# A fused attention and expert step: q and k turned by four transposes, and the score operands laid out by DMAs

## The reference

```python
x = x + 0.5 * ffn(layernorm(x))          # shared expert (2048 wide) and 8 routed experts, top 2
x = x + attn(layernorm(x))
x = x + 0.5 * ffn(layernorm(x))
# attn: groups of 64 tokens, 16 heads of 16 features
q, k, v = split(x @ w_qkv)
q, k = rmsnorm(q) * ln_w, rmsnorm(k) * ln_w
att = softmax(where(causal, q @ k.T / 4, -max))   # per group and head, 64 x 64
y = (att @ v) @ w_proj
```

## Time and profile before

| | before |
|---|---|
| median of three runs | 2153.27 us |
| span of the profiled execution | 2152.2 us |
| PE matmul busy | 2122.4 us |
| PE weight loads busy | 1945.3 us |
| DVE busy | 1428.8 us |
| ACT busy | 1031.8 us |
| POOL busy | 461.3 us |
| DMA moved | 168.41 MB, mean 78 GB/s |

### The profile page before, as it was taken

The page is one execution under the profiler, slowest core; times in us unless marked ns, Lnnn a source line. Parts: engine busy times, 40 slices in busy tenths (PEclk is TensorE's granted clock), DMA queues, the critical chain, the costliest instruction groups (busy, mean ns, idle before and its releaser), DMA issues.

```text
span 2152.2 us, 38420 instructions
## 1 busy us (share of the span) xinstructions
PE 2122.4 (99%) x14228; PEld 1945.3 (90%) x14228; DVE 1428.8 (66%) x3140; ACT 1031.8 (48%) x2006; POOL 461.3 (21%) x440
## 2 busy tenths in 40 slices
PE   9999999999999999999999999999999999999999
PEld 7888899999998888888888888888999999988888
DVE  7666656666665788888888987666466666633333
ACT  4233335555553666666666663333355555532222
POOL 2423211212122222222224322332112121200000
PEclk9999999999999999999999999999999999999999
DMA  9231225564445000000101102221244444441010
GB/s 271 103 110 64 68 74 135 131 148 104 101 112 150 21 2 20 21 20 1 36 1 57 38 11 88 91 83 57 70 104 105 109 104 104 111 135 60 30 59 20
DMA packets 194602, 168.41 MB, mean 78 GB/s; under 512 B 17017, under 2 KB 175149, under 8 KB 194416
## 3 DMA queue, kind: packets, MB, share of 16 engines
q1 hardware_dynamic: 176752, 144.57, 22.5%
q0 software_dynamic: 17664, 21.38, 5.7%
HBM read 104.32 MB, written 68.07 MB: 80 GB/s over the span
## 4 chain that ended last, share of the span: by engine, by line
PE 85%; DVE 9%; issue 3%; ACT 1%; SPq 1%; POOL 0%; DMA 0%; another core or an unknown queue 0%; DVEq 0%; ACTq 0%
PE gate_up_p L339 28%; PE quad L339 24%; PE out_p L377 21%; PE misc L377 4%; PE misc L512 2%; PE quad L529 1%; DVE p_s L1178 1%; PE misc L403 1%; DVE smax L1174 1%; PE quad L543 1%; DVE h_s L1042 1%; PE misc L395 1%; DVE y_s L1187 1%; PE misc L414 1%; PE misc L412 1%
## 5 line engine op out<-in xcount | busy, mean ns | idle before, releaser
L339 PE MATMUL gate_up_p<-zh,w 128*128 128x512 f32 (+2 forms) x2368 | 703.4, 360 | 0.6 <-DVE zl L1346 0.5
L713 ACT CAST hh<-h_s 128x512 fp32r<-128x512 f32 (+2 forms) x511 | 276.3, 541 | 700.4 <-DVE h_s L1042 631.9
L339 PE MATMUL quad<-zh,w 128*128 128x512 f32 (+2 forms) x1728 | 481.8, 346 | 0.0
L339 PEld LDWEIGHTS gate_up_p<-zh,w 128*128 128x128 f32 x2368 | 428.3, 188 | 48.7 <-DVE zl L1346 0.9
L377 PE MATMUL out_p<-w,hh 128*128 128x256 f32 x2808 | 455.5, 281 | 3.3 <-DVE hl L1058 1.9
L377 PEld LDWEIGHTS out_p<-w,hh 128*128 128x128 f32 x2808 | 400.8, 188 | 23.5 <-DVE hl L1058 4.4
L339 PE MATMUL gate_up_p<-zl,w 128*128 128x512 f32 (+2 forms) x1184 | 420.3, 355 | 0.0
L1058 DVE TENSOR_TENSOR hl<-h_s,hh 128x512 fp32r<-128x512 f32 (+2 forms) x431 | 247.2, 574 | 136.4 <-ACT hh L713 118.9
L1042 DVE TENSOR_TENSOR h_s<-gate_up_p,sg_s 128x512 f32<-128x512 f32 (+2 forms) x296 | 178.4, 603 | 236.5 <-PE gate_up_p L339 217.4
L339 PEld LDWEIGHTS quad<-zh,w 128*128 128x128 f32 x1728 | 308.5, 188 | 24.6
L339 PE MATMUL quad<-zl,w 128*128 128x512 f32 (+2 forms) x864 | 295.3, 342 | 0.0
(11 more groups left out here) (201 smaller groups left out, 2747.6 us busy)
## 6 DMA issues: line engine op xcount, KB each, us to landing
stage<-in_L_ffn_rg SPq DMA_DIRECT2D x128, 128.0 KB
stage<-in_L_ffn_ru SPq DMA_DIRECT2D x128, 128.0 KB
stage<-in_L_ffn_rd SPq DMA_DIRECT2D x128, 128.0 KB
slots_d<-empty SPq DMA_DIRECT2D x16, 662.5 KB, 7.5
zh_d<-zh SPq DMA_DIRECT2D x16, 512.0 KB
zl_d<-zl SPq DMA_DIRECT2D x16, 512.0 KB
y_d<-x SPq DMA_DIRECT2D x16, 512.0 KB
zh<-zh_d SPq DMA_DIRECT2D x16, 512.0 KB, 4.1
```

Source lines behind the costliest of these rows:

```text
L339: last = pe.matmul(dst, a, b, start=(k == 0), stop=(k == 3 * n - 1))
L713: nc.scalar.copy(hh[:, n % 2, 0:ncol], h_s[:, n % 2, 0:ncol]).then_inc(sm["hh_done"], 1)
```

## The change

q and k are turned as plain 128 x 128 blocks: four transposes (`head_transposes`) straight from `qk` into `quad` bank 0, after `up` of the same step in which `qk_normal` ran. ACT rounds the bank into `qkh` (`heads_high`, after the cast of the turned probabilities), DVE subtracts for `qkl` (`heads_low`, before `pl`). SP writes both to a scratch in DRAM, eight DMAs per tile, each part where the layout of the score operands has it (q as high, low, high, low and k as high, high, low, low, 16 rows each per head), and loads `k_t` and `q_t` from there by four DMAs once the scores of the tile before are done. The score products keep their number. `qcat`, `kcat`, `twin`, `queries`, both `k_t` copies and POOL's two subtractions go. The scores stand after the second `gate` in every step and wait for the loads and for `heads_low` of the tile that is in stage z, since both use `quad` bank 0. `qk_normal` stands before `values_low` in every step. SP's waits and DMAs of the fused stretch are written out by steps (`fused`), with the saves and loads of heads at the end of each.

```diff
+        heads_d = dram("heads_d", [2, 2, HALF_HEADS, PARTS, HD, C], F32)
...
-        q_t = sb("q_t", [P, NH // 2, 2, P], F32R, att)
-        qcat = sb("qcat", [P, NH, 64], F32, att)
-        kcat = sb("kcat", [P, NH, 64], F32, att)
+        q_t = sb("q_t", [P, NH // 2, 3, GROUP], F32R, att)
+        qkh = sb("qkh", [P, 2, C], F32R, att)
+        qkl = sb("qkl", [P, 2, C], F32R, att)
...
-            def pair_transposes(src, rows, done):
+            def head_transposes(t):
+                pe.wait_ge(sm["a_qn"], t + 1)
+                for j in range(2):
+                    for k in range(KC):
+                        o = j * C + k * P
+                        last = pe.transpose(quad[:, 0, o:o + P], qk[:, j, k * P:(k + 1) * P], ident[:, :])
+                last.then_inc(sm["a_qkt"], 1)
+
+            def prob_transposes(t):
+                pe.wait_ge(sm["a_exp"], t + 1)
+                wait(pe, sm["a_pl"], t)
                 for j in range(NH // 2):
-                    last = pe.transpose(misc[0:rows, j // 4, (j % 4) * P:(j % 4 + 1) * P],
-                                        src[:, 2 * j:2 * j + 2, :].rearrange("p h d -> p (h d)")[:, 0:rows], ident[:, :])
-                last.then_inc(sm[done], 1)
+                    last = pe.transpose(misc[:, j // 4, (j % 4) * P:(j % 4 + 1) * P],
+                                        p_s[:, 2 * j:2 * j + 2, :].rearrange("p h d -> p (h d)"), ident[:, :])
+                last.then_inc(sm["a_pt"], 1)
 
             def scores(t, z, out):
-                pe.wait_ge(sm["a_qe"], t + 1)
-                pe.wait_ge(sm["a_ke0"], t + 1)
-                pe.wait_ge(sm["a_ke1"], t + 1)
+                pe.wait_ge(q_in[t % 2], 32 * (t // 2 + 1))
+                pe.wait_ge(k_in[t % 2], 32 * (t // 2 + 1))
                 if z is not None:
-                    pe.wait_ge(sm["a_qn"], z + 1)
+                    pe.wait_ge(sm["a_qkl"], z + 1)
                     pe.wait_ge(sm["a_vl"], z + 1)
                 if out is not None:
                     pe.wait_ge(sm["a_o"], out + 1)
@@ -526,7 +541,8 @@
                     o = (j % 4) * P
                     for g, rows in ((1, P), (0, GROUP + 2)):
                         own = slice(GROUP * g, GROUP * g + GROUP)
-                        last = pe.matmul(quad[0:rows, j // 4, o:o + P].rearrange("p (r c) -> p r c", r=2), q_t[:, j, g, 0:rows],
+                        last = pe.matmul(quad[0:rows, j // 4, o:o + P].rearrange("p (r c) -> p r c", r=2),
+                                         q_t[:, j, g:g + 2, :].rearrange("p a c -> p (a c)")[:, 0:rows],
                                          k_t[:, j, :, own], start=(g == 1), stop=True, skip_group_check=(g == 0))
                 last.then_inc(sm["a_s"], 1)
 
@@ -552,15 +568,9 @@
...
-                if uses:
-                    pe.wait_ge(sm["misc_free"], max(uses) + 1)
...
-                if keys is not None:
-                    pe.wait_ge(sm["a_qlo"], keys + 1)
-                    wait(pe, sm["a_pl"], keys - 1)
-                    pair_transposes(qcat, QKROWS, "a_qt")
...
-                if keys is not None:
-                    pe.wait_ge(sm["a_qe"], keys + 1)
-                    pair_transposes(kcat, QKROWS, "a_kt")
                 if z is not None:
                     qkv(z, out)
...
                 if probs is not None:
-                    pe.wait_ge(sm["a_exp"], probs + 1)
-                    wait(pe, sm["a_pl"], probs)
-                    if keys is not None:
-                        pe.wait_ge(sm["a_ke0"], keys + 1)
-                        pe.wait_ge(sm["a_ke1"], keys + 1)
-                    pair_transposes(p_s, P, "a_pt")
+                    if uses:
+                        pe.wait_ge(sm["misc_free"], max(uses) + 1)
+                    prob_transposes(probs)
                 if not early_down:
                     up(n, b % 2, c, buf, SB)
-                if keys is not None and c and out is not None:
-                    scores(keys, z, out)
+                if z is not None:
+                    head_transposes(z)
                 loaded(f, phase, b, c + 1)
                 gate(n + 1, b % 2, c + 1, buf, SB)
...
-            heads = lambda ap: ap.rearrange("p (h d) -> p h d", d=HD)
             pairs = misc[:, :, :].rearrange("p b (j c) -> p (b j) c", c=P)
-            high = lambda ap: ap.bitcast(F32R)
-
-            def queries(t, g):
-                own = slice(GROUP * g, GROUP * g + GROUP)
-                act.wait_ge(sm["a_qt"], t + 1)
-                wait(act, sm["a_s"], t)
-                last = nc.scalar.copy(q_t[0:QKROWS, :, g, own], pairs[0:QKROWS, :, own])
-                if g:
-                    last.then_inc(sm["a_qe"], 1)
+
+            def heads_high(t):
+                act.wait_ge(sm["a_qkt"], t + 1)
+                if t:
+                    act.wait_ge(qkh_sv[(t - 1) % 2], 64 * ((t - 1) // 2 + 1))
+                nc.scalar.copy(qkh[:, :, :], quad[:, 0, :].rearrange("p (j c) -> p j c", j=2)).then_inc(sm["a_qkh"], 1)
 
             def values_high(t):
                 act.wait_ge(sm["a_v"], t + 1)
...
-            def twin(t):
-                act.wait_ge(sm["a_qn"], t + 1)
-                wait(act, sm["a_kt"], t)
-                for dst, q, apart in ((qcat, 0, HD), (kcat, 1, 2 * HD)):
-                    twice = dst[:, :, 0:2 * apart].rearrange("p h (n d) -> p h n d", d=apart)[:, :, :, 0:HD]
-                    last = nc.scalar.copy(high(twice), heads(qk[:, q, :]).unsqueeze(2).broadcast_to([P, NH, 2, HD]))
-                last.then_inc(sm["a_qc"], 1)
...
-                if keys is not None:
-                    queries(keys, 0)
...
-                if keys is not None:
-                    queries(keys, 1)
                 silu(n, SB)
-                if keys is not None:
-                    act.wait_ge(sm["a_kt"], keys + 1)
-                    wait(act, sm["a_s"], keys)
-                    nc.scalar.copy(k_t[0:64, :, 0, :], pairs[0:64]).then_inc(sm["a_ke0"], 1)
                 if z is not None:
                     act.wait_ge(sm["a_qk"], z + 1)
                     wait(act, sm["a_qke"], z)
-                    wait(act, sm["a_qlo"], z)
+                    wait(act, sm["a_qkt"], z)
...
+                if z is not None:
+                    heads_high(z)
                 h_high(n, SB)
-                if z is not None:
-                    twin(z)
                 silu(n + 1, SB)
...
-                wait(dve, sm["a_qlo"], t)
+                wait(dve, sm["a_qkt"], t)
...
+            def heads_low(t):
+                dve.wait_ge(sm["a_qkh"], t + 1)
+                if t:
+                    dve.wait_ge(qkl_sv[(t - 1) % 2], 64 * ((t - 1) // 2 + 1))
+                v.tensor_tensor(qkl[:, :, :], quad[:, 0, :].rearrange("p (j c) -> p j c", j=2), qkh[:, :, :],
+                                ALU.subtract).then_inc(sm["a_qkl"], 1)
...
-                if keys is not None:
-                    dve.wait_ge(sm["a_kt"], keys + 1)
-                    wait(dve, sm["a_s"], keys)
-                    v.tensor_copy(k_t[64:128, :, 1, :], pairs[64:128]).then_inc(sm["a_ke1"], 1)
...
-                    if keys is None:
-                        h_product(n, SB)
-                    if c:
-                        values_low(z)
                     qk_normal(z)
-                    if c == 0:
-                        values_low(z)
+                    values_low(z)
                 if not draining:
                     others(s - 1, 1)
-                if keys is not None or draining:
+                if z is not None or draining:
                     h_product(n, SB)
+                if z is not None:
+                    heads_low(z)
...
-                if z is not None:
-                    pool.wait_ge(sm["a_qc"], z + 1)
-                    heads = lambda ap: ap.rearrange("p (h d) -> p h d", d=HD)
-                    g.tensor_tensor(qcat[:, :, 2 * HD:3 * HD].bitcast(F32R), heads(qk[:, 0, :]), qcat[:, :, 0:HD], ALU.subtract)
-                    g.tensor_tensor(kcat[:, :, HD:2 * HD].bitcast(F32R), heads(qk[:, 1, :]), kcat[:, :, 0:HD],
-                                    ALU.subtract).then_inc(sm["a_qlo"], 1)
...
+            def save_heads(t, src, done, landed, parts):
+                par = t % 2
+                sp.wait_ge(done, t + 1)
+                if t >= 2:
+                    sp.wait_ge(q_in[par], 32 * (t // 2))
+                    sp.wait_ge(k_in[par], 32 * (t // 2))
+                for j in range(2):
+                    for part in parts[j]:
+                        sp.dma_start(heads_d[par, j, :, part, :, :],
+                                     src[:, j, :].bitcast(F32)).then_inc(landed[par], 16)
+
+            def load_heads(t):
+                par = t % 2
+                sp.wait_ge(qkh_sv[par], 64 * (t // 2 + 1))
+                sp.wait_ge(qkl_sv[par], 64 * (t // 2 + 1))
+                sp.wait_ge(sm["a_pad"], 3)
+                wait(sp, sm["a_s"], t)
```

(21 more changed lines are left out.)

90 lines of the change are left out of this document (55 added, 35 removed).

## The result

The kernel after took 2166.18 us in the median of four runs (2165.33 to 2174.65), beside 2152.8 of the kernel before: a ratio of 1.0068 [1.0048, 1.0088]. The forecast was 2166. The profiled execution of after has a span of 2163.6 us, 11.4 over the 2152.2 of before.

A forecast was written before the change was run, and what follows sets the result against it. PE was taken to set most of the time, with fused steps a ring through PE and DVE. Terms 9.6, 3.6 and 2.4 less 3 gave plus 12.6 on 2152.2, so a 2166 us median; forecast 2157 to 2175, range 2140 to 2188.

The forecast's parts named there:

- The ring: Fused step: PE's scores, DVE's `masked` through sums of y, next z transpose; with c other than 0, 17.96 to 18.6 us.
- the move behind the gate: Scores always behind the second gate product, now in the ring's part before the scores; start 10.9 us, not 9.78.
- the wait for `heads_low`: Scores wait on DVE's `heads_low` of the tile just transposed, sharing their bank; it was to end at 10.65 us.
- The sign named for the second: Profile after: scores would show idle time before them, waiting for DVE's `heads_low`; no size given.
- c = 0: Fused steps with c = 0: scores at 11.45 us, step 19.2 against 18.61, plus 0.6 in each of 6.
- Contention with POOL: DVE's `hl` no longer slowed by POOL's subtractions: 0.2 us off the ring, 6.26 becoming 6.06.
- The last steps: Last eight steps, DVE also preparing the next layer's blocks: plus 0.3 us each, 2.4, bounds less 0.55 to plus 0.64.
- The ends: Three steps filling and one or two draining the pipeline, no closed ring: minus 3 us in all (0 to minus 5).
- the steps: Full fused steps: 15 with c other than 0 at plus 0.64 us (9.6), 6 with c = 0 at 0.6 (3.6).
- The transfers: Eight stores and four loads per tile, landed by 27.0 us, scores at 29.5: hidden by at least 2.5, cost nothing.
- The clock: TensorE's clock stays at 2.4 GHz, as in a stretch 16.84 us busy of 18; no cost, no chance given.
- Rival A: PE keeps its saving if sums of y are ready when `down` ends: 1.29 us less per step, 2113 us, chance 0.10.

The follow-up runs named there:

- heads_early: Kernel after with head transposes ahead of `up`, their cast and subtraction earlier, and scores ahead of the second gate (c other than 0): ratio 0.9956 to the kernel before.
- before_late: Kernel before with only the scores moved behind the second gate product in every step: ratio 1.0062 to the kernel before.
- after_early: Kernel after with the scores put back ahead of the second gate, where the kernel before has them: ratio 1.0166 to the kernel before.
- after_again: Kernel after, unchanged, run again on the chip of early_filled: ratio 1.0084 to the kernel before.
- more_dma: Kernel after with every store of heads made twice, the second to a scratch nobody reads: ratio 1.0283 to the kernel before.
- early_filled: after_early with six discarded products in PE's wait before the scores, in steps with c other than 0: ratio 1.0073 to the kernel before.
- after_nomax: Kernel after without the row maximum and its subtraction: ratio 0.9938 to the kernel before; the kernel before with the same left out: 0.9875.

## Why the prediction was right, step by step

- **The ring** was read rightly, and its terms came within 0.2 us (forecast, then measured from the step's start): qkv 2.92, 2.96; `up` 7.30, 7.33; head transposes 8.6, 8.60; gate 9.0, 9.16; end of `heads_low` 10.65, 10.78; scores 10.9, 10.96; `masked` 12.55, 12.59; `masked` to the next z 6.06, 5.98; step 18.6, 18.57. heads_early shows the one-to-one tie of `masked` to the step, before_late that the place of the scores is worth the whole.
- **Two holds, not one.** The text priced the move behind the gate and the wait for `heads_low` as one sequence. after_early shows that the second alone gives 18.6, and before_late that the first alone gives 18.7. They cover each other; undoing one brings nothing. The sign named for the second, scores that wait for `heads_low`, is not in the page of after by name: their 0.58 is "issue". `heads_low` ends at 1008.57 and the scores start at 1008.75, and after_early, where the scores wait 1.77 for the same place, is what shows it.
- **c = 0**: forecast 19.2, measured 19.2 to 19.3. The head transposes stood at 9.18 where 9.0 was said, and waited 0.63 for the norm.
- **Contention with POOL**: 0.2 was taken off for `hl`. It takes 0.67 to 0.69 in the whole stretch now, against 0.90 in the earlier trace rows, and from `masked` to the next z it is 0.08 less still than forecast.
- **The last steps**: 2.4 forecast for eight, 1.4 measured for seven; the bound to either side held.
- **The ends**: minus 3 was forecast for the filling and draining steps. The filling steps took 0.5 more, with the first scores waiting 2.54 us for q and the clock at its lower level behind that. The 2.0 that step 5 began earlier is no gain of the change: in after_again it begins at 690.28, 1.3 later than before. Only the drain gave something, 0.9. So this term was wrong in size (minus 0.4 for minus 3), and a chance offset of one execution made up for it in the span. That the forecast met the median within 0.2 us is luck: the ends, the last steps, the offset and the clock are each off by 1 to 5 us, and after_again had a ratio of 1.0084. What was not luck are the steps, 12.3 us for the 13.2 forecast.
- **The transfers** were hidden with 3.9 us to spare where 2.5 at least was said; more_dma bounds it. The q loads, with runs of 256 B, took 0.9 us longer than the k loads issued just before them (4.8 and 3.9), which is no doubling; how much of it is the runs is not shown. The exception, not foreseen, is the first tile.
- **The clock** was called no rival, because a stretch with 16.84 us busy of 18 ran at 1.00. That is the part of the argument that failed, though the forecast did not hang on it. One stretch at 1.00 did not settle it: most of the waits over 2 us in after and after_early are followed by the lower level, but not all (2.20 and 2.27 us in after_early, at 1153.33 and 1265.51, and 3.01 in early_filled are not). In after it is 0.998, at most some 5 us, and how much of that the ring's own waits absorbed is not settled, so a part of the 11.4 may be the clock's. In steps 8 to 28, where 12.3 of it lie, the window of 735 to 1130 us shows 1.00. In after_early the clock took some 15 us, and there it decided.
- **Rival A** needed the sums of y early. after_nomax gives them early and the saving still does not appear: 17.51 against 17.56. So A was priced wrongly by its own condition. A saving on PE shows only if the waits behind it shrink too, as in heads_early.

## What to carry to other kernels

Before pricing a removed instruction, ask what it covers: sixteen transposes that stood over waits for other engines were worth 0.11 us per step at most, until the work they waited beside was moved earlier too. When two things hold an instruction at the same place, undo both. And when an edit leaves PE idle for two microseconds at a time, look at the granted clock in short windows, not at the step alone.

## What the runs showed of the hardware

- The granted clock fell from the 2.4 to the 1.2 GHz level around single waits of PE of 2.23 us (until 1092.47 in after_early) and 2.54 us (until 710.78 in after), with PE busy for 2.98 and 2.95 of the 5 us from 1090 and from 705. It did not fall behind the regular waits of 1.2 to 1.3 us of after's steps 8 to 28, nor behind one of 3.01 us in early_filled. Discarded products in waits of 1.77 us took the mean clock from 0.991 to 0.998 and 15.4 us off the span.
- A subtraction of 512 columns on POOL takes 1.02 us (two in 2.04). DVE's `hl` loses 0.2 beside POOL's subtractions (0.90 against 0.68), and DVE's subtraction of 512 columns takes 2.14 when POOL's on the weights begins 0.24 before it, and 1.15 when it begins first.
